# Loads and three quarters of a norm moved into the block ahead of a self-attention

## The reference, cut to what matters

```
x = x + cross_attention(norm(x), ctx, Wq, Wk, Wv, Wout, bout)
x = x + self_attention(norm(x), Wq, Wk, Wv)      # rotary tables on Q and K, causal mask
...
norm(x) = (x - mean(x)) / sqrt(var(x) + 1e-5)    # over the 512 channels of a token
```

## Time and profile before

| | us |
|---|---|
| median of three runs | 1840.79 |
| lowest and highest of them | 1831.35, 1844.19 |
| the profiled execution | 1835.99 |
| its span, first to last instruction | 1833.7 |
| granted TensorE clock, mean of the span | 0.950 of full |

### The profile page before, as it was taken

How to read it: one execution, slowest core, us unless ns; L and a number is a source line. 1 busy time by engine, 2 the same in 40 slices (tenths; PEclk the granted TensorE clock), 3 DMA queues, 4 the chain that set the end, 5 groups by cost and what they waited for, 6 DMA issues and landing times. The chain is left out here.

```text
span 1833.7 us, 23193 instructions
## 1 busy us (share of the span) xinstructions
PE 1703.6 (93%) x8830; PEld 1316.8 (72%) x8830; DVE 991.7 (54%) x1526; ACT 581.0 (32%) x1054; POOL 339.3 (19%) x294
## 2 busy tenths in 40 slices
PE   7899999999998989987999988989799999999996
PEld 4899999999994777753565656558687665676672
DVE  1669677687673634465899997474523440000014
ACT  4353444443522111112344432034245511111110
POOL 0521432133200010022355542100100020000010
PEclk9899999999998989988798989989898989999998
DMA  4322133213113567736163550430100086696960
GB/s 130 108 91 72 55 108 93 70 54 109 55 40 131 197 246 254 255 117 240 54 223 113 171 208 1 153 140 1 66 28 1 1 286 238 224 341 226 322 233 29
DMA packets 112898, 251.36 MB, mean 137 GB/s; under 512 B 14710, under 2 KB 44294, under 8 KB 108038
## 3 DMA queue, kind: packets, MB, share of 16 engines
q1 hardware_dynamic: 104208, 230.65, 36.3%
q10 hardware_dynamic: 6006, 10.62, 1.7%
q0 software_dynamic: 2560, 8.39, 1.4%
HBM read 230.89 MB, written 18.75 MB: 136 GB/s over the span
## 5 line engine op out<-in xcount | busy, mean ns | idle before, releaser
L374 PE MATMUL x_s_ps<-x_cxt,x_qs 128*128 128x400 f32 (+1 forms) x1152 | 246.0, 359 | 9.5 <-POOL x_qs L347 5.4
L400 PE MATMUL x_o_ps<-x_cx,x_pt 128*128 128x386 f32 (+1 forms) x1248 | 230.3, 343 | 0.0
L1129 PEld LDWEIGHTS e_ps<-e_xg,e_w 128*128 128x128 f32 x1792 | 206.6, 192 | 32.7 <-issue 32.5
L400 PEld LDWEIGHTS x_o_ps<-x_cx,x_pt 128*128 128x128 f32 (+1 forms) x1248 | 220.6, 190 | 1.4
L1129 PE MATMUL e_ps<-e_xg,e_w 128*128 128x128 f32 x1792 | 209.2, 276 | 6.6 <-issue 5.8
L374 PEld LDWEIGHTS x_s_ps<-x_cxt,x_qs 128*128 128x128 f32 x1152 | 207.1, 192 | 10.8 <-issue 10.6
L1121 PE MATMUL e_ps<-e_w,xt 128*128 128x512 f32 x352 | 160.5, 597 | 0.9 <-DMA e_w<-in_L_ffn_W 0.9
L2228 PE MATMUL x_s_ps<-x_cxt,x_qs 128*128 128x512 f32 (+1 forms) x384 | 144.0, 533 | 7.8 <-POOL x_qs L2424 5.8
L2228 PEld LDWEIGHTS x_s_ps<-x_cxt,x_qs 128*128 128x128 f32 x384 | 69.1, 197 | 85.8 <-issue 79.9
L450 DVE TENSOR_TENSOR x_pt<-x_t_ps,x_pt 128x512 fp32r<-128x512 f32 (+1 forms) x128 | 74.7, 586 | 92.6 <-ACT x_pt L540 92.1
L1364 DVE TENSOR_TENSOR e_y<-e_ps,e_b 128x512 f32<-128x512 f32 x20 | 13.7, 686 | 202.7 <-PE e_ps L1121 202.7
(11 more groups left out here) (390 smaller groups left out, 2696.7 us busy)
## 6 DMA issues: line engine op xcount, KB each, us to landing
e_w<-in_L_ffn_W SPq DMA_DIRECT2D x16, 4096.0 KB, 16.2
x_cxt<-in_ctxT SPq DMA_DIRECT2D x8, 2401.5 KB, 8.7
x_cx<-in_ctx SPq DMA_DIRECT2D x8, 2304.0 KB
e_w<-in_L_ffn_gate_up_proj SPq DMA_DIRECT2D x8, 2048.0 KB, 8.1
x_stage<-in_ctxT SPq DMA_DIRECT2D x16, 768.0 KB, 4.4
x_stage<-in_ctx SPq DMA_DIRECT2D x16, 768.0 KB, 6.3
e_w<-in_L_ffn_down_proj SPq DMA_DIRECT2D x8, 1024.0 KB, 8.8
ff_w<-in_L_xattn_W SPq DMA_DIRECT2D x2, 4096.0 KB, 17.2
```

The source lines that it names most:

```text
L374: last = nc.tensor.matmul(s_ps[:, n, 0:b - a], qs[:, u % 2, p, c, :], cxt[:, q, c, a:b], start=(m + c == 0), stop=(m + c == len(PARTS) + C ...
L400: last = nc.tensor.matmul(o_ps[:, 0:WIDE], pt[0:rows, p, t, :], cx[0:rows, q, t, :], start=(t + m == 0), stop=(t + m == KT - 1 + len(PARTS ...
L1129: last = nc.tensor.matmul(u_ps[:, g % 2, a * PER + n, :], w1[:, e % PAIR, m, a * hidden + c * P:a * hidden + (c + 1) * P], xg[:, m, :], st ...
```

## The change

The weights, tables and mask of the self-attention get a class, `SelfWeights`, whose tiles lie on the other side of the on-chip memory and live through both blocks. Their six loads are issued in the last block of the cross-attention, behind `wout` and `bout`. The norm is now a `BlockNorm`, which goes block by block. For blocks 0 to 2 VectorE takes statistics and aggregation right behind the add of y and makes their rows there, GpSimd the deviation. Block 3 is left to the self-attention's block, where VectorE subtracts the first weight tile between its aggregation and its row. TensorE transposes blocks 0 to 2 first, and the 14 idle transposes stand ahead of block 3.

```diff
+class BlockNorm(Norm):
+
+
+    def feed(self, dve, t):
+        V = self.core.nc.vector
+        V.bn_stats(self.stats[:, t, :], self.src[:, t, :]).then_inc(self.stats_ready, 1)
+        dve.wait_ge(self.stats_ready, t + 1)
+        V.bn_aggr(self.mv[:, t, :], self.stats[:, t, :]).then_inc(self.mv_ready, 1)
+
+    def begin(self, pool):
+        self.core.nc.gpsimd.memset(self.half[:, :], -0.5).then_inc(self.rstd_ready, 1)
+
+    def deviation(self, pool, t):
+        G, one = self.core.nc.gpsimd, slice(t, t + 1)
+        pool.wait_ge(self.mv_ready, t + 1)
+        G.tensor_scalar_add(self.var[:, one], self.mv[:, t, 1:2], EPS).then_inc(self.rstd_ready, 1)
+        pool.wait_ge(self.rstd_ready, 2 * t + 2)
+        G.tensor_tensor(self.rstd[:, one], self.var[:, one], self.half[:, one], ALU.pow).then_inc(self.rstd_ready, 1)
+
+    def scaled(self, dve, t):
+        dve.wait_ge(self.mv_ready, t + 1)
+        dve.wait_ge(self.rstd_ready, 2 * t + 3)
+        self.core.nc.vector.tensor_scalar(self.normed[:, t, :], self.src[:, t, :], self.mv[:, t, 0:1], self.rstd[:, t:t + 1],
+                                          ALU.subtract, ALU.mult).then_inc(self.normed_ready, 1)
...
-def cross_attention_L0(core, normalise, x, xn, xt, k, ident, w):
+def cross_attention_L0(core, normalise, hold, x, xn, xt, k, ident, w):
...
+            after = SelfWeights(core, hold, w)
+            norm = BlockNorm(core, hold, "n1", x, xn, side="right")
             with nc.Block() as block:
                 @block.sync
                 def _(sp):
                     sp.dma_start(wout[:, :, :], w["L0_xattn_Wout"].rearrange("(c p) n -> p c n", p=P)).then_inc(wout_in, 16)
                     sp.dma_start(bout[:, :], bcast(w["L0_xattn_bout"])).then_inc(bout_in, 16)
+                    after.load(sp)
+
+                @block.gpsimd
+                def _(pool):
+                    norm.begin(pool)
+                    for t in range(TT - 1):
+                        norm.deviation(pool, t)
 
                 @block.tensor
...
-                        nc.vector.tensor_tensor(x[:, t, :], x[:, t, :], y_ps[:, t, :], ALU.add)
+                        nc.vector.tensor_tensor(x[:, t, :], x[:, t, :], y_ps[:, t, :], ALU.add).then_inc(x_ready, 1)
+                        if t < TT - 1:
+                            dve.wait_ge(x_ready, t + 1)
+                            norm.feed(dve, t)
+                        if 1 <= t < TT - 1:
+                            norm.scaled(dve, t - 1)
+                        if t == TT - 2:
+                            norm.scaled(dve, t)
+    return after, norm
...
+class SelfWeights:
+
+
+    def __init__(self, core, ctx, w):
+        self.w = w
+        self.wqk = core.sb(ctx, "s0_wqk", [P, 2, KC, D], side="right")
+        self.wv = core.sb(ctx, "s0_wv", [P, KC, D], side="right")
+        self.tables = core.sb(ctx, "s0_tables", [P, 2, KC // 2, TOK], side="right")
+        self.mask = core.sb(ctx, "s0_mask", [P, P], side="right")
+        self.in_q, self.in_k, self.in_v, self.in_tab, self.in_mask = core.sems(ctx, "s0l", "in_q in_k in_v in_tab in_mask")
+
+    def load(self, sp):
+        w = self.w
+        for slot, name, s in ((0, "L0_attn_Wq", self.in_q), (1, "L0_attn_Wk", self.in_k)):
+            sp.dma_start(self.wqk[:, slot, :, :], w[name].rearrange("(c p) n -> p c n", p=P)).then_inc(s, 16)
+        for a, name in enumerate(("rope_cos", "rope_sin")):
+            sp.dma_start(self.tables[:, a, :, :], w[name].rearrange("(c p) n -> p c n", p=P)).then_inc(self.in_tab, 16)
+        sp.dma_start(self.wv[:, :, :], w["L0_attn_Wv"].rearrange("(c p) n -> p c n", p=P)).then_inc(self.in_v, 16)
+        sp.dma_start(self.mask[:, :], w["mask_L0"]).then_inc(self.in_mask, 16)
...
             @block.sync
             def _(sp):
-                for slot, name, s in ((0, "L0_attn_Wq", in_q), (1, "L0_attn_Wk", in_k)):
-                    sp.dma_start(wqk[:, slot, :, :], w[name].rearrange("(c p) n -> p c n", p=P)).then_inc(s, 16)
-                for a, name in enumerate(("rope_cos", "rope_sin")):
-                    sp.dma_start(tables[:, a, :, :], w[name].rearrange("(c p) n -> p c n", p=P)).then_inc(in_tab, 16)
-                sp.dma_start(wv[:, :, :], w["L0_attn_Wv"].rearrange("(c p) n -> p c n", p=P)).then_inc(in_v, 16)
-                sp.dma_start(mask[:, :], w["mask_L0"]).then_inc(in_mask, 16)
                 sp.wait_ge(zero_ready, 1)
...
             @block.gpsimd
             def _(pool):
-                norm.inverse_deviation(pool)
+                norm.deviation(pool, TT - 1)
                 nc.gpsimd.memset(zero[:, :], 0.0).then_inc(zero_ready, 1)
 
             @block.tensor
             def _(pe):
-                for n in range(IDLE):
-                    nc.tensor.transpose(tps[:, TT - 1, n % KC, :], ident[:, :], ident[:, :])
                 for t in range(TT):
+                    if t == TT - 1:
+                        for n in range(IDLE):
+                            nc.tensor.transpose(tps[:, t, n % KC, :], ident[:, :], ident[:, :])
                     pe.wait_ge(norm.normed_ready, t + 1)
                     for c in range(KC):
                         last = nc.tensor.transpose(tps[:, t, c, :], xn[:, t, c * P:(c + 1) * P], ident[:, :])
...
-                norm.statistics(dve)
-                norm.rows(dve)
+                norm.feed(dve, TT - 1)
+                weight_low(0)
+                norm.scaled(dve, TT - 1)
                 for t in range(TT):
-                    weight_low(t)
+                    if t:
+                        weight_low(t)
```

More of the change, by code:

```diff
@@ L75, with __init__ @@
 class Norm:
-    def __init__(self, core, ctx, name, src, normed, gamma=None, beta=None):
+    def __init__(self, core, ctx, name, src, normed, gamma=None, beta=None, side="left"):
         self.core, self.src, self.normed, self.gamma, self.beta = core, src, normed, gamma, beta
[L80 to L84, removed]
+        self.stats = core.sb(ctx, f"{name}_stats", [P, TT, 6], side=side)
+        self.mv = core.sb(ctx, f"{name}_mv", [P, TT, 2], side=side)
+        self.var = core.sb(ctx, f"{name}_var", [P, TT], side=side)
+        self.half = core.sb(ctx, f"{name}_half", [P, TT], side=side)
+        self.rstd = core.sb(ctx, f"{name}_rstd", [P, TT], side=side)
         self.stats_ready, self.mv_ready, self.rstd_ready, self.normed_ready = core.sems(
@@ L609, in _, with self_attention_L0 @@
                         dve.wait_ge(xb_ready, t + 1)
-                        nc.vector.tensor_tensor(x[:, t, :], x[:, t, :], y_ps[:, t, :], ALU.add)
-def self_attention_L0(core, x, xn, ident, w, sent, back):
+                        nc.vector.tensor_tensor(x[:, t, :], x[:, t, :], y_ps[:, t, :], ALU.add).then_inc(x_ready, 1)
[23 more added lines that the diff above has]
+        sp.dma_start(self.mask[:, :], w["mask_L0"]).then_inc(self.in_mask, 16)
+def self_attention_L0(core, x, xn, ident, weights, norm, sent, back):
     nc = core.nc
@@ L620, in self_attention_L0 @@
     ORDER = (0, 2, 1, 3)
+    wqk, wv, tables, mask = weights.wqk, weights.wv, weights.tables, weights.mask
+    in_q, in_k, in_v, in_tab, in_mask = weights.in_q, weights.in_k, weights.in_v, weights.in_tab, weights.in_mask
     with ExitStack() as ctx:
-        wqk = core.sb(ctx, "s0_wqk", [P, 2, KC, D])
-        wv = core.sb(ctx, "s0_wv", [P, KC, D])
         qks = core.sb(ctx, "s0_qks", [P, 2, 2, KC, D], F32R)
@@ L635, in self_attention_L0 @@
         zero = core.sb(ctx, "s0_zero", [P, D])
-        norm = Norm(core, ctx, "n1", x, xn)
         ps = core.pb(ctx, "s0_ps", [P, 8, 512])
         tps = ps[:, 4:8, :].rearrange("p t (c n) -> p t c n", c=KC)
-        zero_ready, zeroed, in_q, in_k, in_v, in_tab, in_mask, t_ready, xh_ready, xl_ready, wh_ready, wl_ready, vh_ready, vl_ready = core.sems(
-            ctx, "s0w", "zero_ready zeroed in_q in_k in_v in_tab in_mask t_ready xh_ready xl_ready wh_ready wl_ready vh_ready vl_ready")
+        zero_ready, zeroed, t_ready, xh_ready, xl_ready, wh_ready, wl_ready, vh_ready, vl_ready = core.sems(
+            ctx, "s0w", "zero_ready zeroed t_ready xh_ready xl_ready wh_ready wl_ready vh_ready vl_ready")
         qk_ready, prod_ready, rot_ready, v_ready, v_copied, s_ready, sm_ready, max_ready, exp_ready, inv_ready, p_ready, pt_ready, y_ready = \
@@ L2921, in norm @@
             return lambda ahead=None: norm_stage(core, name, x, xn, xt, ident, ahead=ahead)
-        cross_attention_L0(core, norm("n0"), x, xn, xt, k, ident, w)
-        self_attention_L0(core, x, xn, ident, w, sent, back)
+        with ExitStack() as hold:
+            weights, norm_s0 = cross_attention_L0(core, norm("n0"), hold, x, xn, xt, k, ident, w)
+            self_attention_L0(core, x, xn, ident, weights, norm_s0, sent, back)
         moe_L0(core, x, xn, xt, w, sent, back)
```

5 lines of the change are left out of this document (2 added, 3 removed).

## The result

The changed kernel takes 1827.54 us (median of 8 runs, 1816.1 to 1831.97), the kernel before 1840.65 us (8 runs, 1831.35 to 1844.19). The ratio of the two is 0.9937, with a 95% interval of 0.9909 to 0.9964: between 6.6 and 16.8 us faster. The forecast of 1831.5 lies 4.0 above, and within its range of 1823 to 1841. The profiled execution took 1831.12 us with a span of 1829.3 us.

What follows compares the result with a forecast made beforehand. Self-attention's projections were held by late weight loads, with the norm next, and ran partly at a lower clock. 5.3 + 2.84 - 1.1 - 0.1 = 6.9 us off a base of 1838.4 gave 1831.5 us, range 1823 to 1841.

Steps and rivals of the forecast that it cites:

- The late start: Start of the self-attention's block: moved loads and norm let the first projection matmul start at 586.4 against 591.69, 5.3 us earlier.
- Both ends meet: Ahead of block 3's transposes: its norm row (584.95) and TensorE's earlier and idle transposes (about 585.0) end together.
- the slower pair: GpSimd's addition of EPS and pow for block 3, taken at 0.42 and 0.86 us with 0.08 between, ending at 584.26.
- The new wait: After eight projection matmuls TensorE waits for VectorE's low part of x: 1.1 us lost, bounds 0 and 1.6.
- The clock: Q and K's 96 matmuls no longer partly run at the 1.2 GHz level: 2.84 us gained.
- I take it that the clock stays up: Assumption that TensorE, with only some tenths of idling and the 1.1 us wait, keeps full clock: 2.84 us gained.
- the rival: Clock falls all the same in Q and K: gain only 2.9 us, time 1835.5 us; 20%.
- The last add: End of the cross-attention's last block: last add of y late by 0 to 0.2 us behind block 2's row; 0.1 taken.
- The rest at nothing: Wout's load, scratch fillings, projections to the end and what follows the value matmuls: no change in time.
- The sign of being wrong: Forecast wrong if the following MoE block, moved against its own loads, takes another length.
- The Trainium skill's rule: Shared port lock would delay GpSimd's block 3 deviation from 582.9 to 583.5, sum 6.6 us; sum left at 6.9.
- The rivals: Clock falls anyway (20%, 1835.5 us); loads delay Wout (7%, 1835.1); lower clock stays through Q and K (5%, 1839.4 to 1852.1).

Runs made afterwards that it cites:

- r4: Changed kernel with VectorE's low parts and ScalarE's casts of x ahead of later weight tiles; 26.24 us from block start to first value matmul, whole kernel 0.9938 of before.
- r5: Kernel before plus 52 unread transposes filling TensorE's waits in the self-attention's block; first value matmul at 31.73 us, whole kernel 0.9977 of before.
- r6: Changed kernel without the 14 idle transposes of the self-attention's block; first projection at 4.33 us, first value matmul at 27.31, clock 1.00 in Q and K.
- r12: Kernel before, unchanged, profiled a third time (the third profile of before); first projection at 9.54 us, first value matmul at 33.06, clock 0.93 in Q and K.
- r7: Changed kernel with the six loads issued ahead of Wout and bout; first value matmul at 27.28 us, but 33.50 instead of 27.29 us from first Wv matmul to the block.
- r8: r4 with the first weight tile's subtraction moved behind block 3's row; first projection at 4.14 us, first value matmul at 26.03.
- r11: Kernel before, unchanged, profiled a second time; first projection at 9.59 us, first value matmul at 34.26, clock 0.88 in Q and K.
- r1: Changed kernel, unaltered, profiled and timed a second time; first value matmul at 27.29 us, whole kernel 0.9956 of before.
- r10: Changed kernel, unaltered, profiled and timed a third time; first value matmul at 27.29 us, whole kernel 0.9930 of before.

## Why the prediction was right

Point by point, by its own steps:

- **The late start, 5.3 us.** Measured 9.78 - 4.34 = 5.44. "Both ends meet" held: block 3's transposes began at 3.01 us, the idle ones ended at 3.03. GpSimd's chain took 1.20 us from 580.37, not the 1.36 I took from the slower pair: pow on one column is 0.56, on two it was 0.72 and 0.86, while the addition had the wait for the subtraction in it.
- **The new wait, 1.1 us.** Measured 1.05, after eight matmuls, ended by the row named. r4 removed it and gained 1.05.
- **The clock, 2.84 us.** The first profile of before gives 34.33 - 27.32 = 7.01 = 5.44 - 1.05 + 2.62 for it, and r5 alone 2.60. The 0.2 short of the forecast is the pace: 96 matmuls at the full clock took 21.89 us (r5), not 21.7. The step "I take it that the clock stays up" held in all three profiles of the changed kernel and in the five variants built on it that kept both halves. It was an assumption, and the ground I gave against the rival doesn't carry it: the "three microseconds of idling in five ahead of the fall" are 2.3 by the rows, and r6 had 2.8 without a fall. What I didn't see is that the kernel before pays less in some executions (r12: 23.52 against 21.89, 1.6 us).
- **The last add, 0.1 us.** Nothing. Pow on one column was shorter than I had allowed, so the row of block 2 was out of the way just when the add's turn came.
- **The rest at nothing.** Held: Wout landed after 5.5 us, and the next block came 20.0 us after the value matmul. r7 shows what the cover is: the place in the queue, worth 4.5 us of waiting and 1.7 of clock. The sign of being wrong that I gave for the mixture's block, another length, can't be read in these runs: up to the next cross-attention's first matmul it takes 188.5 to 196.0 us in the changed kernel, but 195.0 in the third profile of before too.
- **The Trainium skill's rule.** The Trainium skill, "SBUF — State Buffer", section "🔬 SBUF: two separate sides", has VectorE and GpSimd share a port pair as an exclusive lock. The trace agrees, with the addition ending 0.07 us behind the subtraction's end, and back at 0.21 us in r8 with nothing beside it. I had read the 0.3 us in the earlier trace rows as a stretch and less than a whole operation; with an addition that ends as the other engine's operation does, a lock met in its middle is the better reading. Its price at block 3's row is the 0.35 us of r8. The sum was hardly touched, since the stretch I had allowed was about as long.
- **The rivals.** In none of the profiles with both halves in place did the clock fall between the block's start and the first value matmul. Wout wasn't held. No lower level of 16 us or more came in Q and K.

The sum to the value matmul was 6.9 us and 7.0 were measured. That it came so close is in part luck: the start gave 0.14 more, the wait and the add cost 0.15 less, the clock gave 0.2 less, and the first profile of before was one with a long lower level; against the third the gain is 5.8. The median moved by 13.1. I had the scatter only as "A single median of this kernel moves by a few microseconds"; four medians of the kernel before lie between 1835.44 and 1840.65 and three of the changed one between 1820.06 and 1827.98. The forecast of 1831.5 started from a base 2.2 us under the median of before and took a drop 6.2 us smaller than measured, and so ended 4.0 too high. The range up to 1841 would have held an unchanged kernel too (1840.65), so it is the profile and not the median that bears the mechanism out. The three ratios together say 10.8 us.

## What to carry to other kernels

Where two things that an engine waits for are late by nearly the same, neither moved alone gives much and both together give all (the start came 2, 0 and 5.4 us earlier here): look for the second behind the first before judging a move. Loads for the next stage cost nothing in this one as long as they are issued behind what this stage still needs; the same loads ahead of it cost 6.2 us. And a wait that goes can give back the matmuls' clock behind it, here 1.6 to 2.7 us of a gain of 5.8 to 7.0, depending on the profile of before that it is held against.

## What the runs showed of the hardware that was not expected

- The clock stayed at 1.00 through waits of 1.05, 1.50 and 0.68 us one soon after another (r6), and in r11 it fell behind idle times of 1.66 and 0.66 with 1.1 us of transposes between them. In r12 the same kernel passed the same idle times without a fall, which came 5 us later. The filler of 14 transposes made no difference to the changed kernel.
- GpSimd's addition on one column, 0.21 to 0.25 us alone, took 0.44 beside VectorE's row of the norm and 0.56 beside its subtraction, and both times it ended 0.07 to 0.08 us behind the other's end; pow on one column took 0.56 to 0.58 in every place, in r8 beside VectorE's subtraction with one operand in PSUM.
- Two profiles of one and the same kernel (r1, r10) differ by 22 us behind the same point, with the same instructions.
